# Larger ScalarE pieces, sums mixed with cosines on TensorE and earlier row scales in an arccos attention with mixture of experts

## The reference, cut to what matters

```python
q, k = l2norm(heads(q)), l2norm(heads(k))
cos = einsum('bhsd,bhtd->bhst', q, k)
g_dist = arccos(clip(cos, -1 + EPS, 1 - EPS))
attn_score = (1 + g_dist) ** (-3.2)
n_r, n_c = attn_score.sum(-1), attn_score.sum(-2)
k_tilde = n_r**-1 [:, None] * attn_score * n_c**-1 [None, :]
probs = k_tilde / maximum(k_tilde.sum(-1), 1e-12)
x = x + (probs @ v) @ w_out.T + b_out
x = x + u + routed(u) + shared(u)      # u = layernorm(x); 16 experts of which 2 count, and 2 shared ones
```

## Time and profile before

| | |
|---|---|
| median of 3 executions | 5255.96 us (5255.17 to 5260.99) |
| the profiled execution's own time | 5259.16 us |
| its span, first to last instruction | 5257.5 us |
| ScalarE busy | 4840.3 us, 92% |
| VectorE busy | 4119.0 us, 78% |
| TensorE matmuls busy | 3091.0 us, 59% |
| GpSimd busy | 1806.5 us, 34% |
| mean granted TensorE clock | 0.744 of 2.4 GHz |

### The profile page before, as it was taken

How to read it: one execution, slowest core, us unless ns; L and a number is a source line. 1 busy time by engine, 2 the same in 40 slices (tenths; PEclk the granted TensorE clock), 3 DMA queues, 4 the chain that set the end, 5 groups by cost and what they waited for, 6 DMA issues and landing times. The chain is left out here.

```text
span 5257.5 us, 37245 instructions
## 1 busy us (share of the span) xinstructions
PE 3091.0 (59%) x10544; PEld 799.1 (15%) x10678; DVE 4119.0 (78%) x3989; ACT 4840.3 (92%) x1263; POOL 1806.5 (34%) x545
## 2 busy tenths in 40 slices
PE   8645555554565455545546565555655565565699
PEld 4200011100010000000011111111111111111244
DVE  7767878777787777777778888887888888887566
ACT  5799999999999999999989999999999999999421
POOL 0224443344433444334423443334433443334000
PEclk9866676667666665776677868686878868686799
DMA  2200000000000000000000101010100101010200
GB/s 89 64 8 14 18 18 14 10 18 18 18 14 18 10 10 10 10 6 6 12 29 26 34 26 36 12 43 10 46 16 26 34 26 36 14 40 2 84 31 13
DMA packets 71846, 128.17 MB, mean 24 GB/s; under 512 B 9654, under 2 KB 46937, under 8 KB 71706
## 3 DMA queue, kind: packets, MB, share of 16 engines
q1 hardware_dynamic: 70554, 122.50, 7.3%
q0 software_dynamic: 1152, 4.19, 0.3%
HBM read 96.77 MB, written 29.88 MB: 24 GB/s over the span
## 5 line engine op out<-in xcount | busy, mean ns | idle before, releaser
L1156 POOL TENSOR_TENSOR X<-X 128x2048 f32<-128x2048 f32 x504 | 1798.0, 3602 | 2929.6 <-DVE X L957 2929.6
L816 PE MATMUL psum<-stacks 128*128 128x512 bf16 x3962 | 1630.5, 503 | 848.8 <-DVE X L971 442.7
L971 DVE TENSOR_TENSOR X<-psum,X 128x1024 f32<-128x1024 f32 x1024 | 1191.0, 1217 | 417.7 <-ACT X L1188 381.0
L978 DVE TENSOR_REDUCE ncol<-X 128x4 f32<-128x8192 f32 x128 | 1111.4, 8683 | 373.4 <-ACT X L1208 367.3
L841 PE MATMUL psum<-X,vp 128*32 128x512 f32 x4096 | 704.6, 851 | 1172.9 <-DVE vp L984 1172.9
L957 DVE TENSOR_SCALAR X<-psum 128x1024 f32<-128x1024 f32 x1024 | 1191.0, 1216 | 35.2 <-DVE rows L1078 24.7
L1196 ACT ACTIVATE X<-X 128x4096 f32<-128x4096 f32 (+1 forms) x192 | 898.0, 4740 | 22.2 <-DVE X L971 22.2
L1188 ACT ACTIVATE X<-X 128x4096 f32<-128x4096 f32 x256 | 904.8, 3605 | 0.7
L1180 ACT ACTIVATE X<-X,consts 128x8192 f32<-128x8192 f32 x128 | 903.8, 7108 | 0.0
L1208 ACT ACTIVATE X<-X 128x8192 f32<-128x8192 f32 x128 | 892.8, 7022 | 2.0
L1204 ACT ACTIVATE X<-X,consts 128x16384 f32<-128x16384 f32 x64 | 892.9, 13951 | 0.8
(11 more groups left out here) (165 smaller groups left out, 1110.2 us busy)
## 6 DMA issues: line engine op xcount, KB each, us to landing
V<-expert_w SPq DMA_DIRECT2D x64, 512.0 KB, 3.6
stacks<-qk_parts SPq DMA_DIRECT2D x256, 64.0 KB
qk_parts<-X SPq DMA_DIRECT2D x96, 128.0 KB, 1.9
stacks<-qk_parts SPq DMA_DIRECT2D x64, 192.0 KB
head_out<-evac SPq DMA_DIRECT2D x32, 256.0 KB, 2.1
expert_w<-u_t SPq DMA_DIRECT2D x17, 256.0 KB, 2.6
X<-in_L_attn_x_dram POOLq DMA_DIRECT2D x8, 512.0 KB, 4.3
stacks<-qk_parts SPq DMA_DIRECT2D x32, 128.0 KB
```

The costliest lines, as they stand in the source:

```text
L816: return nc.tensor.matmul(dst, stacks[:, 1, buf, keys:keys + P], stacks[:, 0, buf, q0:q0 + n], start=True, stop=True)
L971: nc.vector.tensor_tensor(part, ps_cos[j % 2], part, ALU.mult).then_inc(cos_ok, 1)
L978: nc.vector.reduce_sum(ncol[:, a:b], X[:, m % 2, a:b, :], AX.X).then_inc(sums_ok, 1)
L1156: nc.gpsimd.tensor_tensor(own, own, own, ALU.mult).then_inc(square_ok, 1)
```

## The change

1. LOG_PIECES becomes one piece of eight tiles, and HALF_PIECES three pieces of 2, 3 and 3 tiles. The waits follow: the only Ln of a unit waits for all eight squares, and the products of tiles 2 to 4 and 5 to 7 wait for the second and the third Sigmoid.
2. On TensorE the last four `add` of a unit are mixed with the cosines of tiles 1 to 4 of the next unit.
3. `side_scales` goes ahead of the clips of unit 34, from behind them. The residual stays behind the clips.
4. Both row scales are made by two VectorE instructions in place of five: max(nrow x TINY, den), then its reciprocal. SCALE_STEPS follows.

```diff
-        LOG_PIECES = ((0, 4), (4, 8))
-        HALF_PIECES = ((0, 2), (2, 4), (4, 6), (6, 8))
+        LOG_PIECES = ((0, 8),)
+        HALF_PIECES = ((0, 2), (2, 5), (5, 8))
...
                     if has(k, m + 1):
                         mult(k, m + 1, 0)
-                    for i in range(BT):
+                    for i in range(BT // 2):
                         add(k, m, i)
+
+                    for i in range(BT // 2, BT):
+                        add(k, m, i)
+                        if has(k, m + 1):
+                            mult(k, m + 1, i - BT // 2 + 1)
                     if has(k, m + 1):
-                        for i in range(1, BT):
+                        for i in range(BT // 2 + 1, BT):
                             mult(k, m + 1, i)
...
-                SCALE_STEPS, PAIR_STEPS = 4, 24
+                SCALE_STEPS, PAIR_STEPS = 1, 24
...
                     dve.wait_ge(side_sums, 32)
-                    link(nc.vector.reciprocal(side_nrow, side_nrow))
-                    link(nc.vector.tensor_tensor(side_den, side_den, side_nrow, ALU.mult))
-                    link(nc.vector.tensor_scalar_max(side_den, side_den, TINY))
-                    link(nc.vector.reciprocal(side_den, side_den))
-                    nc.vector.tensor_tensor(side_scl, side_den, side_nrow, ALU.mult).then_inc(side_scl_ok, 1)
+                    link(nc.vector.scalar_tensor_tensor(side_den, side_nrow, TINY, side_den, ALU.mult, ALU.max))
+                    nc.vector.reciprocal(side_scl, side_den).then_inc(side_scl_ok, 1)
...
+                    if starts(k, m):
+                        side_scales()
+                        assert steps[0] == SCALE_STEPS
                     for i in range(BT):
                         if has(k, m + 2):
                             clip(k, m + 2, i)
...
                     if starts(k, m):
-                        side_scales()
-                        assert steps[0] == SCALE_STEPS
                         side_work(k, m)
...
                 dve.wait_ge(t_sums, 64)
-                link(nc.vector.reciprocal(nrow, nrow))
-                link(nc.vector.tensor_tensor(den, den, nrow, ALU.mult))
-                link(nc.vector.tensor_scalar_max(den, den, TINY))
-                link(nc.vector.reciprocal(den, den))
-                nc.vector.tensor_tensor(scl, den, nrow, ALU.mult).then_inc(scale_ok, 1)
+                link(nc.vector.scalar_tensor_tensor(den, nrow, TINY, den, ALU.mult, ALU.max))
+                nc.vector.reciprocal(scl, den).then_inc(scale_ok, 1)
```

## The result

The changed kernel took 5288.89 us (median of 5 executions, 5287.47 to 5290.3) against 5260.72 for the kernel before (5 executions, 5255.17 to 5270.15): ratio 1.0052, 95% interval 1.0041 to 1.0063. It is slower by half a per cent. The profiled execution took 5287.47 us, its span is 5285.8, 28.3 more than before. That was forecast in sign and in mechanism; the forecast size was +15, about half of what came.

The account below looks back on a forecast made before the run. ScalarE, busy 92% of the span, was taken as the bound. Terms -17.9 + 41 + 34.7 - 22.2 - 17.8 - 2.5 = +15.3 us gave 5271 us against the median of 5255.96, 0.29% slower; range 5243 to 5303.

Parts of the forecast that it names:

- ScalarE pieces: On ScalarE, one Ln for two and three Sigmoids for four save 0.28 us a unit over 64 units: 17.9 us off.
- One Ln waits: In 22 units of the second half, the squares' whole lateness becomes a ScalarE wait: plus 41 us, ends 30 and 50.
- Mixing: On TensorE, mixed sums delay Arctan 0.55 us in 63 units, plus 34.7; old waits in 12 late-sum units end, minus 22.2.
- Scales ahead of the clips: First row scales, earlier and shorter: ScalarE's 18.15 us wait in unit 33 goes, 0.3 comes back at unit 34: minus 17.8.
- Last scales: Last row scales at the kernel's end take 2.3 us in place of 4.78: minus 2.5 us.
- free mixing: Rival: clock rises early in each mixed run on TensorE, Arctan waits 0.1 us a unit, 6 in all; 5243 us; 20%.
- the earlier squares: Rival: higher clock in second-half clips and side matmuls brings squares earlier, Ln waits 25 in place of 41; 5249 us; 12%.
- the clock did rise within the mixed run: Judges the rival that TensorE's clock never rises in the mix, a 2.3 us wait each unit; 5416 us; 6%.
- the scales brought their 18 us: Judges the rival that the early first row scales don't bring their 18 us (residual or unit 34's squares late); 5289; 10%.

Follow-up runs that it names:

- the filler: Changed kernel with eight idle-time matmuls, results unused, on TensorE behind the fifth sum of units 0 to 31: 5272.9 us, ratio 1.0022.
- the run with the sums first: Changed kernel with all eight sums ahead of the cosines again, so no mixing: 5269.56 us, ratio 1.0020.

## Why the prediction was right, and where its sizes were off

- **ScalarE pieces, -17.9.** Measured -11.6 for the Ln (903.8 to 892.2) and -5.9 for the Sigmoids (904.8 to 898.9). Right.
- **One Ln waits, +41.** Alone it was 40.9. In the changed kernel it was 46.9 in 23 units. This is the term that was mis-sized: I had set the gain from a higher clock against products that end later, and called it even; the products won, by 5.9 us. Over the 22 late units the last products end 7.9 us later in all and the squares 5.0, so the work between them gave some back, as I had hoped, and not enough. With neither mixing nor larger Sigmoids the waits were 40.9, with three Sigmoids and the early scales but no mixing 51.4, with the mixing and four Sigmoids 48.9, with all of it 46.9. So in the changed kernel the mixing alone is enough for the later squares, and the three Sigmoids add nothing to them; where the mixing was gone, squares came 5.8 us later with three Sigmoids than in the run with four, and the other 4 us are a ScalarE that came to its Ln earlier. The room before Arctan did hide their 0.49 us, but the path to the squares of the next unit has no room in the second half.
- **Mixing, +34.7 and -22.2.** Measured 33.9 in place of 22.2, so +11.7 for a forecast +12.5. The mechanism (low clock at the start, up after 3.5 to 6 us, 0.1 to 0.95 us a unit) was borne out by the windows and by the filler; the ends measured are 0 and 1.2. Late sums no longer held VectorE for long, also as forecast: its longest wait for cosines before a product is 1.7 us and was 3.5. One premise was thinner than I took it: cosines alone had stayed at the low clock in the earlier trace rows, but in unit 33 of the same trace cosines alone, with the same gaps, saw the clock rise after 3 us.
- **A term that was missing, about +5.** Without a wait, ScalarE's next instruction starts 0.09 us before the last one has ended: in the earlier trace rows the Sigmoids end at 2060.82 and Arctan starts at 2060.73. A wait breaks that. There are 72 waits at these two lines now and were 12, 60 x 0.09 = 5.4 us, and no idle column shows them.
- **Scales ahead of the clips, -17.8.** Right: the 18.15 us went, the clips covered the way through memory, the instruction took 0.67 with GpSimd idle, and unit 34's Ln waited 0.56, for an expected 0.3.
- **Last scales, -2.5.** Measured -1.1: 2.57 saved, 1.47 given back as a longer wait for the DMA. I had taken a chain that everything waits for as if its next link had a fixed length.

The measured terms make -17.5 + 46.9 + 11.7 + 5.4 - 18.15 - 1.1 = +27.3, against 28.3 of span; about 1 us is not placed. The forecast's 15.3 differs mainly by the squares (5.9), the broken overlaps (5.4) and the last scales (1.4).

Of the rivals, free mixing and the earlier squares did not happen, the clock did rise within the mixed run in every unit from 1 to 63, and the scales brought their 18 us. Matmuls kept program order: cosines stood behind a sum of 1.93 us while VectorE waited for them. The Trainium skill, TensorE: Matmul & The Clock Gate, section Part 2: What happens when you issue a matmul, says that matmuls stay in program order and only weight loads are pulled ahead, and the trace agrees.

## What to carry to other kernels

A larger piece saves its fixed cost in every unit and pays with the wait for its last input; look up, unit by unit, when that last input arrives, and split only where it is late: the same edit was worth 0.18 us where the input was early and cost about 2 us (1.3 to 3.2, but for one unit) where it was late. What interleaving two streams on TensorE costs was decided here by the clock at the start of the run, not by the mean of the kernel, so do it only where the stream that it moves was really in the way: the same mixing cost 23 us in one half of the kernel and gained 6 in the other. Room measured at one consumer is not room at the next: in the run with the sums first, products that end half a microsecond later cost nothing before Arctan and went on to the squares that the Ln waits for.

## What was not expected of the hardware

- Cosines alone, with 0.19 us between every four of them, ran for 18 us at a granted clock of 0.54, while mixed with the sums, without gaps, they saw it rise after 3 to 6 us. It is not always so: in unit 33 of the kernel before, cosines alone with the same gaps of 0.19 us ran at 0.50 from 2633.2 to 2636.2 and at 1.00 from there. What separates the two cases no run shows. Once up, it stayed up with cosines of 0.60 us every 1.13 us, and in the filler's run it had fallen after a gap of 3.61 us.
- ScalarE's back-to-back instructions overlap by 0.09 us, and a wait of any length costs that on top.
- The profile's idle time for a wait is therefore short of its cost: 80.8 us of idle at the two lines cost about 87.
- A VectorE instruction on two tensors of 512 elements, both in SBUF (the on-chip memory beside PSUM), took 0.67 to 0.69 us with GpSimd idle, and 1.88 (L1012) and 2.88 (L1001) while GpSimd was squaring. With one of them in PSUM it took 0.69 (L1014 of the changed kernel, at 2691.74) though GpSimd was squaring.
